# Splitting the expert weights inside the softmax attention, and both layer norms' factors from one power

## The reference

```
h = emb(x) + pos
h = h + attention1(layernorm(h))            # 8 heads, causal, normalized dot products, no softmax
hx = layernorm(layernorm(h)) * ln_g + ln_b  # the outer norm, then the block's own
q, k, v = hx @ Wq, hx @ Wk, hx @ Wv         # 2 heads of 64; q and k are l2-normalized
o = softmax(causal(q @ k.T)) @ v
y = o @ Wo;  gate = softmax(y @ gate_W + gate_b)
hid = gelu(y @ W1[e] + b1[e]);  eo = hid @ W2[e] + b2[e]     # 8 experts, FF = 512
out = h + sum over e of gate[e] * eo[e]
```

## Time and profile before

| | |
|---|---|
| median of 3 runs | 964.44 us (957.14 to 966.6) |
| the profiled execution's own time | 964.4 us |
| its span | 962.3 us |
| busy in the span: PE, DVE, ACT, POOL | 86%, 76%, 53%, 38% |
| mean granted TensorE clock | 0.919 |

### The profile page before, as it was taken

One profiled execution on the slowest core, in us unless ns is written; L12 is line 12 of the kernel. 1 busy time (PEld: TensorE's weight loads), 2 busy tenths in 40 slices (PEclk: granted clock), 3 DMA queues, 4 the chain that ended last, 5 costly groups with the idle time before them and its releaser, 6 DMA issues.

```text
span 962.3 us, 21449 instructions
## 1 busy us (share of the span) xinstructions
PE 827.2 (86%) x7864; PEld 592.4 (62%) x7864; DVE 732.0 (76%) x1725; ACT 513.4 (53%) x1069; POOL 366.6 (38%) x478
## 2 busy tenths in 40 slices
PE   1677999999667565888898998699999999999997
PEld 1555777777433333556665666477777777777775
DVE  5736666666579896667667774399999999999997
ACT  1322444444056765667686898455555555555553
POOL 7565555555567774455565676100000000000000
PEclk9887999999656766899999999799999999999999
DMA  3110000000001110000000000000000000000000
GB/s 124 46 26 4 1 0 0 0 0 0 1 22 43 33 41 16 1 1 2 2 2 1 2 2 2 1 2 13 2 12 2 13 3 11 13 2 13 2 13 12
DMA packets 9474, 11.65 MB, mean 12 GB/s; under 512 B 1832, under 2 KB 6704, under 8 KB 9264
## 3 DMA queue, kind: packets, MB, share of 16 engines
q1 hardware_dynamic: 8368, 8.43, 2.9%
q0 software_dynamic: 1024, 2.10, 0.8%
HBM read 8.43 MB, written 2.10 MB: 11 GB/s over the span
## 4 chain that ended last, share of the span: by engine, by line
PE 60%; DVE 11%; POOL 11%; issue 9%; ACT 7%; DMA 0%; DVEq 0%; POOLq 0%; ACTq 0%
PE ps L897 59%; POOL plo L359 3%; DVE mx L794 2%; DVE y L684 2%; ACT phi L520 2%; POOL h_all L221 2%; ACT p L519 1%; POOL rr L306 1%; POOL rr L315 1%; DVE x L726 1%; DVE ss L732 1%; POOL ss L323 1%; ACT ql L506 1%; ACT arena L408 1%; PE ps L1167 0%
## 5 line engine op out<-in xcount | busy, mean ns | idle before, releaser
L897 PE MATMUL ps<-y,arena 128*128 128x512 f16 (+1 forms) x896 | 247.4, 424 | 19.3 <-DVE y L684 17.0
L548 ACT ACTIVATE cst<-ps,col 128x512 f32<-128x512 f32 x256 | 176.1, 688 | 163.6 <-PE ps L897 163.6
L897 PEld LDWEIGHTS ps<-arena,sq 128*128 128x128 f16 x3072 | 192.8, 98 | 60.5 <-DVE sq L883 0.7
L897 PE MATMUL ps<-arena,sq 128*128 128x128 f16 x3072 | 213.0, 219 | 0.5 <-DVE sq L883 0.5
L883 DVE TENSOR_TENSOR sq<-cst,sq 128x512 f16<-128x512 f32 x256 | 175.7, 686 | 4.4
L359 POOL TENSOR_TENSOR plo<-p,phi 128x512 f16<-128x512 f32 (+2 forms) x120 | 124.8, 1058 | 89.8 <-ACT phi L520 88.2
L878 DVE CAST sq<-cst 128x512 f16<-128x512 f32 x256 | 108.0, 422 | 12.2 <-ACT cst L548 3.1
L897 PEld LDWEIGHTS ps<-y,arena 128*128 128x128 f16 (+1 forms) x896 | 75.4, 112 | 58.5 <-issue 24.8
L794 DVE TENSOR_REDUCE mx<-ps 128x1 f32<-128x512 f32 (+3 forms) x160 | 91.3, 604 | 24.6 <-PE ps L897 23.8
L519 ACT ACTIVATE p<-ps 128x512 f32<-128x512 f32 (+3 forms) x160 | 88.2, 552 | 23.8 <-PE ps L897 22.6
L520 ACT ACTIVATE phi<-ps 128x512 f16<-128x512 f32 (+3 forms) x160 | 88.7, 554 | 0.0
(11 more groups left out here) (153 smaller groups left out, 1305.8 us busy)
## 6 DMA issues: line engine op xcount, KB each, us to landing
sq<-w_rows SPq DMA_DIRECT2D x16, 256.0 KB, 2.7
out<-h_all SPq DMA_DIRECT2D x32, 64.0 KB, 1.6
cst<-consts SPq DMA_DIRECT2D x1, 1294.0 KB
h_all<-emb_rows,idx POOLq DMA_INDIRECT x32
wqkv<-w_qkv SPq DMA_DIRECT2D x1, 192.0 KB
wsm<-w_sm SPq DMA_DIRECT2D x1, 192.0 KB
row<-rows SPq DMA_DIRECT2D x1, 140.0 KB
c<-consts SPq DMA_DIRECT2D x1, 96.0 KB
```

Source lines behind the costliest of these rows:

```text
L548: a.activation(hid[:, f], ps[:, HBANK[f], :], ACT.Gelu_apprx_tanh, bias=col[:, K_B1 + k:K_B1 + k + 1], scale=1.0 / WS).then_inc(S["hid_rea ...
L897: return t_.matmul(o, l, r, start=start, stop=stop, skip_group_check=True)
```

## The change

Layer norms: VectorE computes v(1 + e) + e*e in `two_norms` (a tensor_scalar of 128 x 2) into `rr[:, 0]`, and GpSimd's `both_norms` is one power. `two_norms(c+3)` stands in VectorE's `step_a2` behind `low_qk(c)`, ahead of `low_v(c+1)`; in the prologue right behind `stats2`.

Weights: `weights_high` and `weights_low` leave `step_a2` on ScalarE and GpSimd. In the softmax attention, at the steps k = 6, 14, ..., 126, ScalarE makes the high half of piece n in one pass behind the step's exponentials (and behind `max_row`, if there is one), and VectorE makes the low half with one scalar_tensor_tensor, stage * WS - high, behind the step's `row_max` and `plo` and ahead of `head_out`. The scaled copy is gone. SyncE stages piece n when the low half of piece n-2 is done. The first two pieces are staged at the same place as before.

```diff
-            with sp.Fori(2, NT - 1, 2) as n:
-                for u in range(2):
-                    sp.wait_ge(S["scaled_ready"], n + (u - 1))
-                    sp.dma_start(stage[u], w12_rows[:, ds(n * 512 + u * 512, 512)]).then_inc(S[STAGED[u]], 16)
+            for n in range(2, NPIECE):
+                sp.wait_ge(S["wlow_ready"], n - 1)
+                sp.dma_start(stage[n % 2], w12_rows[:, n * 512:(n + 1) * 512]).then_inc(S[STAGED[n % 2]], 16)
...
             def both_norms(c, par):
                 pool.wait_ge(S["stats2"], c + 1)
-                k = 5 * c
-                var = mv2[par][:, :, 1]
-                a, b_, c_ = rr[par][:, 0], rr[par][:, 1], rr[par][:, 2]
-                g.tensor_tensor(a, var, ln_eps, ALU.add).then_inc(S["rr_link"], 1)
-                pool.wait_ge(S["rr_link"], k + 1)
-                g.tensor_tensor(b_, a, mhalf[:, 0:B], ALU.pow).then_inc(S["rr_link"], 1)
-                pool.wait_ge(S["rr_link"], k + 2)
-
-                g.tensor_tensor(a, var, b_, ALU.mult).then_inc(S["rr_link"], 1)
-                pool.wait_ge(S["rr_link"], k + 3)
-                g.tensor_tensor(c_, a, b_, ALU.mult).then_inc(S["rr_link"], 1)
-                pool.wait_ge(S["rr_link"], k + 4)
-                g.tensor_tensor(c_, c_, ln_eps, ALU.add).then_inc(S["rr_link"], 1)
-                pool.wait_ge(S["rr_link"], k + 5)
-                g.tensor_tensor(a, c_, mhalf[:, 0:B], ALU.pow).then_inc(S["rn_link"], 1)
-                pool.wait_ge(S["rn_link"], c + 1)
-                g.tensor_tensor(rr[par][:, 3], a, b_, ALU.mult).then_inc(S["rr_ready"], 1)
+                g.tensor_tensor(rr[par][:, 1], rr[par][:, 0], mhalf[:, 0:B], ALU.pow).then_inc(S["rr_ready"], 1)
...
-            def weights_low(c, par):
-                pool.wait_ge(S["scaled_ready"], c + 1)
-                piece = w12[:, ds(c * 4, 4), :, :]
-                g.tensor_tensor(piece[:, :, 1, :], scaled[par].rearrange("p (w d) -> p w d", d=D), piece[:, :, 0, :],
-                                ALU.subtract).then_inc(S["split_done"], 1)
...
-                weights_low(c, par)
...
-            def weights_high(c, par):
-                act.wait_ge(S[STAGED[par]], 8 * (c - par) + 16)
-                act.wait_ge(S["split_done"], c + 1)
-                st = stage[par].rearrange("p (w d) -> p w d", d=D)
-                a.activation(w12[:, ds(c * 4, 4), 0, :], st, ACT.Copy, scale=WS)
-                a.activation(scaled[par], stage[par], ACT.Copy, scale=WS).then_inc(S["scaled_ready"], 1)
+            def weights_high(n):
+                act.wait_ge(S[STAGED[n % 2]], 16 * (n // 2 + 1))
+                a.activation(w12[:, 4 * n:4 * n + 4, 0, :], stage[n % 2].rearrange("p (w d) -> p w d", d=D),
+                             ACT.Copy, scale=WS).then_inc(S["whigh_ready"], 1)
...
                     if k + 2 in FIRST:
                         max_row(FIRST.index(k + 2))
+                    if k in WSLOT:
+                        weights_high(WSLOT.index(k))
...
+            def two_norms(c, par):
+                dve.wait_ge(S["agg2"], c + 1)
+                v.tensor_scalar(rr[par][:, 0], mv2[par][:, :, 1], 1.0 + LN_EPS, LN_EPS * LN_EPS, ALU.mult, ALU.add
+                                ).then_inc(S["stats2"], 1)
...
                 low_qk(c)
+                if left >= 3:
+                    two_norms(c + 3, 1 - par)
                 if left >= 1:
                     low_v(c + 1, 1 - par)
...
+            def weights_low(n):
+                piece = w12[:, 4 * n:4 * n + 4]
+                dve.wait_ge(S["whigh_ready"], n + 1)
+                v.scalar_tensor_tensor(piece[:, :, 1, :], stage[n % 2].rearrange("p (w d) -> p w d", d=D), WS,
+                                       piece[:, :, 0, :], ALU.mult, ALU.subtract).then_inc(S["wlow_ready"], 1)
...
                     v.tensor_tensor(plo[:, k % PR, lo:], p32[:, k % QR, lo:], phi[:, k % PR, lo:], ALU.subtract
                                     ).then_inc(S["plo_dve"], 1)
+                if k in WSLOT:
+                    weights_low(WSLOT.index(k))
...
+WSLOT = [8 * n + 6 for n in range(2 * E * FF // 512)]
```

More of the change, by code:

```diff
@@ L129, in tower @@
         mv2 = [sb(f"mv2{i}", [P, B, 2]) for i in range(2)]
-        rr = [sb(f"rr{i}", [P, 4, B]) for i in range(2)]
+        rr = [sb(f"rr{i}", [P, 2, B]) for i in range(2)]
         x2 = [sb(f"x2{i}", [P, B, D]) for i in range(2)]
@@ L151, in tower @@
         stage = [sqf[:, 0:512], sqf[:, 512:1024]]
-        scaled = [sqf[:, 1024:1536], sqf[:, 1536:2048]]
-        oT, y32 = scaled
+        oT, y32 = sqf[:, 1024:1536], sqf[:, 1536:2048]
         hid = cst[:, C_POS:C_POS + 4 * CH].rearrange("p (u t) -> p u t", u=4)
@@ L160, in tower @@
         ps = ctx.enter_context(nc.psum_tensor("ps", [P, 8, 512], F32))
-        names = """load_c load_w load_s load_stage load_stage1 split_done gathered0 gathered1 gathered setup stats veps
+        names = """load_c load_w load_s load_stage load_stage1 whigh_ready wlow_ready gathered0 gathered1 gathered setup stats veps
             rstd hb_ready xn_ready xnT_ps xn0_sb xsT_sb x0_link qkT_ps qkT_sb qkv_ps qkv_sb dt_ps
@@ L165, in tower @@
             aoT_sb pr_ps h1_ready attn0 attnT0_ps attnT0_sb front_link core_link direct_link pos_ready stats2
-            st2_link rr_link rr_ready x2_ready x2T_ps hxT_sb qkv2_ps sqqk ss_ready rn_link rn_ready qkn_ready
+            st2_link agg2 rr_ready x2_ready x2T_ps hxT_sb qkv2_ps sqqk ss_ready rn_ready qkn_ready
             vhi_ready vlo_ready qkd_ps hi_ready lo_ready sm_ps sm_used max_link mneg mrow_ps mrow_sb s_ps
-            p_ready plo_pool plo_dve scaled_ready pv_done o_link o_used oT_ps oT_sb y_ps yhi_ready ylo_ready
+            p_ready plo_pool plo_dve pv_done o_link o_used oT_ps oT_sb y_ps yhi_ready ylo_ready
             lg_ps lg_link lg_ready eg_ready gate_ready gT_ps gT_sb b2_ps h2_ready hid_ps hid_ready hhi_ready
@@ L348, in _ @@
                     step_a2(c + u, u)
-            for c in range(NT - 4, NT):
+            for c in range(NT - 4, NT - 1):
                 step_a2(c, c % 2, NT - 1 - c)
@@ L493, in step_a2 @@
                     normed_T(c + 2, par)
-                weights_high(c, par)
             with act.Fori(0, NT - 5, 2) as c:
@@ L556, in _ @@
             for i, (name, size) in enumerate([("hid_ready", RING), ("w2_done", RING), ("hlo_even", 2), ("hlo_odd", 2),
-                                              ("eo_used", 8), ("qkn_ready", 1), ("lo_ready", 1), ("vlo_ready", 1),
-                                              ("split_done", 2)]):
+                                              ("eo_used", 8), ("qkn_ready", 1), ("lo_ready", 1), ("vlo_ready", 1)]):
                 v.memset(credit[:, i:i + 1], 0.0).then_inc(S[name], size)
@@ L720, in stats2 @@
                     last = v.bn_aggr(mv2[par][:, b], st2[:, par, b])
-                last.then_inc(S["stats2"], 1)
+                last.then_inc(S["agg2"], 1)
+            def two_norms(c, par):
+                dve.wait_ge(S["agg2"], c + 1)
+                v.tensor_scalar(rr[par][:, 0], mv2[par][:, :, 1], 1.0 + LN_EPS, LN_EPS * LN_EPS, ALU.mult, ALU.add
+                                ).then_inc(S["stats2"], 1)
             def normed2(c, par):
@@ L726, in normed2 @@
                     last = v.tensor_scalar(x2[par][:, b], h_all[:, ds(2 * c + b, 1), :].rearrange("p a d -> p (a d)"),
-                                           mv2[par][:, b, 0:1], rr[par][:, 3, b:b + 1], ALU.subtract, ALU.mult)
+                                           mv2[par][:, b, 0:1], rr[par][:, 1, b:b + 1], ALU.subtract, ALU.mult)
                 last.then_inc(S["x2_ready"], 1)
@@ L760, in _ @@
             stats2(0, 0)
+            two_norms(0, 0)
             variances(NT - 1, 1)
             stats2(1, 1)
+            two_norms(1, 1)
             normed2(0, 0)
@@ L767, in _ @@
             stats2(2, 0)
+            two_norms(2, 0)
             normed2(1, 1)
@@ L861, in _ @@
             dve.wait_ge(S["lg_link"], 5 * B * NQ)
-            dve.wait_ge(S["split_done"], 2 + NPIECE)
+            dve.wait_ge(S["wlow_ready"], NPIECE)
             def add_rows(n, r):
@@ L1176, in _ @@
                         bank4 = S["h2_ready"], m + 1
-            pe.wait_ge(S["split_done"], 2 + NPIECE)
+            pe.wait_ge(S["wlow_ready"], NPIECE)
             pe.wait_ge(S["ylo_ready"], B * NQ)
```

## The result

The changed kernel takes 976.58 us (median, 974.01 to 978.78) against 964.44 us for the kernel before in the same comparison; the ratio is 1.0123, 95% interval 1.009 to 1.0157. One more execution of the kernel before took 1418.27 us, in a slow state, and is left out. The changed kernel is slower by 1.2%, where 960.5 and no difference were forecast, and lies outside the range of 950 to 970. The profiled execution took 978.8 us, its span is 976.9.

The account below looks back on a forecast made before the run. It took the second layer norm's GpSimd-VectorE loop as the bound to relieve, tied with a TensorE-ScalarE loop at half clock. That stage's -8.9 us and the attention's +5.0 gave -3.9: from 964.4 to 960.5 us, range 950 to 970.

Parts of the forecast that it names:

- the two loops: Second layer norm: GpSimd-VectorE loop at 6.92 us an iteration hides TensorE-ScalarE loop at 6.91; afterwards VectorE's 5.6 at high clock.
- Front, -8.9 us: Second layer norm stage shorter by 8.9 us: 1.9 ahead of the loop, 6.5 in it, 0.5 in the last iterations.
- The 1.9 us of the first both_norms: Ahead of the second layer norm's loop, the first call stands alone on the chain: 2.83 - 0.9 = 1.9 us saved.
- An iteration with half of it fast: Second layer norm's loop: an iteration half at the high clock gains about 0.9 us.
- Part 2: Weights out of the second layer norm stage: GpSimd loses 1.15 us an iteration, and x its block (1.54 to 0.60).
- Part 3, ScalarE: +4.6: Attention: ScalarE's sixteen added passes cost 0.4 us at ten item-boundary slots (4.0) and 0.1 at six others (0.6).
- Part 3, VectorE: Attention: sixteen added operations of 0.69 us, waiting for ScalarE ahead of other VectorE work, cost 0.4 us in all.
- Rival E: Attention: VectorE's new operation and GpSimd block each other, 0.9 us per piece reaching TensorE, 14.4 us; 969.9 us, chance 0.18.
- C: Attention: the weight pieces are absorbed at a cost of 1 us; 956.5 us, chance 0.18.
- D: Second layer norm: the slow TensorE-ScalarE loop holds throughout, so the stage gives only 2.4 us; 967.0 us, chance 0.14.
- Rival B: Second layer norm: the clock rises with the shorter iteration and stays, each iteration gaining 1.33 us; 949.7 us, chance 0.12.
- the bound of 19 us for the attention: Attention: upper bound on the added cost if neither engine's work is covered, 16 x (0.52 + 0.69).

Follow-up runs that it names:

- filler: slot7 plus three float16 matmuls per chunk on TensorE in the second stage, their result unused; 950.83 us, ratio 0.9875 to the kernel before.
- slot7: The changed kernel with all sixteen weight pieces one attention step later (8n + 7); 958.89 us, ratio 0.9952 to the kernel before.
- low_last: The changed kernel with VectorE's low half moved to the end of its step, pieces at the same steps; 958.28 us, ratio 0.9974 to the kernel before.
- six_moved: The changed kernel with only the six pieces that share a step with the gate's second part moved one step later; 958.29 us, ratio 0.9977 to the kernel before.
- norms_only: The kernel before with two_norms and the one power, the weights left in the second stage; 954.61 us, ratio 0.9921 to the kernel before.
- no_low: The changed kernel without VectorE's sixteen low-half operations, the low halves set to zero by GpSimd; 956.74 us, ratio 0.9954 to the kernel before.
- ten_moved: The changed kernel with only the ten pieces that don't meet the gate's second part moved one step later; 978.57 us, ratio 1.0185 to the kernel before.

## Why the prediction was wrong

- **What bounds the kernel, the two loops.** Right. GpSimd all but left the chain, and the loop of TensorE and ScalarE took over at 6.7 to 6.85 us (forecast 6.91), VectorE's at 5.6 us where the clock was high (5.57 in the changed kernel, 5.60 in filler).
- **Front, -8.9 us.** Near in the profiled pair, -7.5 us from the first hxT to the first p, with a mean clock of 0.72 against 0.67, and in part by luck. The terms are not what was measured. The 1.9 us of the first both_norms came to 0.7: from the first aggregate to the first hxT it is 4.03 us instead of 4.75, because x stands in VectorE's program behind the next chunk's statistics. An iteration with half of it fast was put at 0.9 us less than 6.92, and in the changed kernel five at 0.74 or 0.75 are 0.2 us shorter. And the clock of this stage is not stable: with the same code the stretch of hxT was 104.9 us in slot7 and 100.7 in the changed kernel. Over many executions the front is worth less than in the pair: slot7, low_last and six_moved, with the same front and no excess in the attention, are 0.9 to 1.5 us faster than the kernel before in their medians.
- **Part 2.** Half right: x was freed, but the one power alone did that (0.37 us in norms_only). The prediction booked it to the weights' move.
- **Part 3, ScalarE: +4.6.** Wrong, 0 (no_low, ten of sixteen pieces in six_moved).
- **Part 3, VectorE: "I take 0.4 us in all".** This is the step that failed: 20 to 21 us in the profiles, about 18 in the medians (976.58 against 958.3 to 958.9). The text named the added wait and what stands behind it (row_max, plo, head_out), and left out the gate, whose second part is in the same step of VectorE's loop. It also weighed the wait by VectorE's idle 91 us. Idle time in sum says nothing of one place: TensorE's transposes stand in program order before the next scores and need that one VectorE result at once. I had placed the pieces against the item boundaries and never against YAT + 4 YGAP; the steps can be counted from `plan()` and all six coincide.
- **Rival E** gave the right side (969.9) with the wrong cause. VectorE's new operation takes 0.69 to 1.51 us, mean 0.875 instead of 0.69, the long ones where they overlap an operation of GpSimd, so the mutual blocking with GpSimd is there, 16 x 0.18 = 3 us of VectorE's time. It is not the cause: low_last and six_moved have it as well (mean 0.85, up to 1.5 us) and their attention is not longer, and ten_moved has the whole excess with next to none of it (mean 0.71, at most 0.79). In slot7 it is absent (0.68 to 0.69). The Trainium skill's rule (SBUF — State Buffer, Who interferes with whom) is thus seen in the durations, and no time here shows a price for it.
- **Rivals C and D.** C (the attention absorbs the pieces) is what slot7, low_last and six_moved show, once no piece stands ahead of the gate. D (the slow loop throughout) is what the profiled slot7 shows: iterations of 6.85 us at 0.50 from 275 to 350 us.
- **Rival B** (a clock that rises) was the wrong reading of this change, but filler shows that the prize existed: 8 us.
- **The range**: its upper end came from 16 equal pieces. Six places at 3.5 us were in no case of it. Rival E came to 14.4 us, and the bound of 19 us for the attention (964.4 - 8.9 + 19 = 974.5) was not carried into the range.

## What to carry to other kernels

A wait that is put into an engine's program costs what stands behind it in that program, so list every consumer in the same step of an unrolled schedule, the rare ones as well (here a gate every 8 to 32 steps), and count the collisions before pricing them; one step's shift, or moving the instruction to the end of its step, can be worth 2% of the kernel. When a stall goes, look for the loop that is tied with it: here a second loop stood within 0.02 us of the first, and two edits that each shorten the first loop don't add up. Where one profile of a stage is compared with one other, look first how much the stage differs between profiles of the same code. And where TensorE stands at the half clock in a stage with gaps, filling them is worth a try: it paid here.

## What the runs showed of the hardware

The granted clock of a stage with gaps is no constant of the code. The same second stage ran at a mean of 0.52 (slot7), 0.60 (six_moved) and 0.72 to 0.73 (the changed kernel, ten_moved) over windows of 97 to 103 us, and its iterations took 6.85 us at 0.50 and 5.57 at 1.00, with values from 6.0 to 6.8 between. Three useless matmuls in TensorE's gaps brought 0.89, and 8 us for the whole kernel. The Trainium skill (TensorE: Matmul & The Clock Gate, Why this matters for your kernels) advises keeping TensorE busy without gaps; filler agrees with it. And a wait of TensorE in the attention costs more than its length: each of the six waits of 2.6 to 3.5 us was followed by transposes of 1.01 us, where five of the six took 0.60 in the kernel before, behind waits of 0.8 to 1.9 us. The six waits grew by 10.0 us (7.9 to 17.8), the attention by 21.2, of which 9.2 are TensorE's same work at a lower clock.
